# Relative-position attention with routed experts on one core: operand images in DRAM, one window transfer per quarter, and a new order of transfers

## The reference, cut to what matters

```python
attn = jnp.einsum('bhid,bhjd->bhij', q, k)
attn = attn + jnp.take_along_axis(qL, idx, axis=-1)          # idx = clip(j - i, -31, 31) + 31
attn = attn + jnp.swapaxes(jnp.take_along_axis(kL, idx, axis=-1), 2, 3)
attn = jax.nn.softmax(attn, axis=-1)
out = jnp.einsum('bhij,bhjd->bhid', attn, v)
# plus segment sums of attn by distance, times rpe_v_table; then w_proj and b_proj
```

## Time and profile before

| | us |
|---|---|
| median of 3 runs | 1705.66 (1693.27 to 1722.01) |
| the profiled execution | 1722.62 |
| its span, first to last instruction | 1720.6 |
| PE busy | 1439.5 (84%) |
| DVE busy | 1142.8 (66%) |
| ACT busy | 802.8 (47%) |
| POOL busy | 537.8 (31%) |

### The profile page before, as it was taken

The page is one execution under the profiler, slowest core; times in us unless marked ns, Lnnn a source line. Parts: engine busy times, 40 slices in busy tenths (PEclk is TensorE's granted clock), DMA queues, the critical chain, the costliest instruction groups (busy, mean ns, idle before and its releaser), DMA issues.

```text
span 1720.6 us, 69484 instructions
## 1 busy us (share of the span) xinstructions
PE 1439.5 (84%) x29626; PEld 962.7 (56%) x29626; DVE 1142.8 (66%) x2468; ACT 802.8 (47%) x1408; POOL 537.8 (31%) x557
## 2 busy tenths in 40 slices
PE   3792788888888889888898888889898888888887
PEld 1341355555555566555567555555565555555565
DVE  7782667777777677677644666665765766665672
ACT  1341245555555455444531545554554555454554
POOL 3462111222222222212333333333333433332333
PEclk9995578888998888888965988886987998888999
DMA  3553656665565555455544656665655665556552
GB/s 86 146 165 121 188 164 187 192 192 177 172 189 172 179 166 169 150 178 159 183 147 116 206 158 175 173 175 169 181 172 148 191 179 169 158 166 173 168 135 87
DMA packets 271582, 283.20 MB, mean 165 GB/s; under 512 B 55033, under 2 KB 205682, under 8 KB 271456
## 3 DMA queue, kind: packets, MB, share of 16 engines
q1 hardware_dynamic: 259984, 274.86, 52.5%
q0 software_dynamic: 11472, 6.83, 2.8%
HBM read 171.49 MB, written 112.36 MB: 165 GB/s over the span
## 4 chain that ended last, share of the span: by engine, by line
PE 50%; DMA 17%; DVE 12%; issue 9%; POOL 5%; SPq 4%; ACT 2%; DVEq 1%; another core or an unknown queue 0%; POOLq 0%; ACTq 0%
PE PS L721 43%; DMA dq_s<-dq_d 9%; DMA dq_d<-dq_e 7%; DVE tops L1505 6%; PE PS L992 5%; POOL ajp L681 3%; DVE dq_s L1546 2%; POOL ajp L679 2%; SPq L424 1%; SPq L478 1%; ACT PT L1190 1%; SPq L545 1%; PE PS L977 1%; PE PS L953 1%; ACT dq_e L1209 0%
## 5 line engine op out<-in xcount | busy, mean ns | idle before, releaser
L1505 DVE TRANSPOSE_TENSOR_REDUCE tops<-PS 128x16 f32<-128x512 f32 x1024 | 697.1, 701 | 377.2 <-PE PS L721 349.7
L1190 ACT ACTIVATE PT<-PS 128x512 f32<-128x512 f32 x1024 | 591.8, 596 | 569.2 <-PE PS L721 561.2
L721 PE MATMUL PS<-Q,K 73*32 73x512 bf16 (+28 forms) x11904 | 714.3, 348 | 140.8 <-issue 83.1
L721 PEld LDWEIGHTS PS<-Q,K 73*32 73x32 bf16 (+1 forms) x11904 | 322.1, 105 | 357.3 <-issue 171.1
L662 POOL COPY WP<-PT 128x768 f32<-128x768 f32 x128 | 105.3, 822 | 954.9 <-PE PS L721 940.8
L721 PE MATMUL PS<-PT,Vst 128*9 128x256 f32 (+7 forms) x7552 | 361.0, 308 | 2.6 <-issue 1.9
L721 PE MATMUL PS<-WT,eye 96*32 96x96 bf16 (+2 forms) x4352 | 294.8, 218 | 1.5 <-issue 1.3
L721 PEld LDWEIGHTS PS<-PT,Vst 128*9 128x9 f32 x7552 | 192.5, 98 | 84.9 <-issue 20.9
L721 PEld LDWEIGHTS PS<-WT,eye 96*32 96x32 bf16 x4352 | 185.8, 106 | 28.7 <-issue 3.2
L992 PE MATMUL PS<-ident,dq_s 127*128 127x127 f32 x512 | 108.6, 351 | 64.4 <-DMA dq_s<-dq_d 61.5
L681 POOL TENSOR_TENSOR ajp<-dq_s,ajp 128x508 bf16<-128x508 f32 x128 | 147.6, 1153 | 10.5
(11 more groups left out here) (207 smaller groups left out, 1051.8 us busy)
## 6 DMA issues: line engine op xcount, KB each, us to landing
aj_d<-ajp SPq DMA_DIRECT2D x64, 768.0 KB
WT<-aj_d SPq DMA_DIRECT2D x768, 64.0 KB, 2.0
dq_d<-dq_e SPq DMA_DIRECT2D x64, 512.0 KB
dq_s<-dq_d SPq DMA_DIRECT2D x64, 512.0 KB
TOE<-toe_d SPq DMA_DIRECT2D x33, 768.0 KB
Q<-q_stack SPq DMA_DIRECT2D x128, 96.0 KB
K<-k_stack SPq DMA_DIRECT2D x128, 96.0 KB
q_stack<-PT SPq DMA_DIRECT2D x24, 256.0 KB, 2.5
```

The costliest lines, as they stand in the source:

```text
L721: return pe.matmul(o, l, r, start=start, stop=stop, skip_group_check=True)
L1190: act.activation(PT[:, TILE + N * J + 512 * half:TILE + N * J + 512 * half + 512], PS[:, 2 + u % 2, :], ACT.Exp).then_inc(s2_read, 1)
L1505: dve.tensor_reduce(tops[:, (h + 1) % 2, s // 2, 16 * (s % 2):16 * (s % 2) + 16], PS[:, s % 2, :].rearrange("p (c i) -> p c i", i=TILE), A ...
```

## The change

1. **Row images.** `q_img` and `k_img` replace the stacks and the far tables. Each holds 60 rows per head, among them rows of ones and of products, in the order in which the operands `Q1`, `K1`, `Q2`, `K2` need them. A pass's rows are now two transfers of 60 rows, not five, and ACT issues them, at slots 1 and 7. The stores of the prologue are 16 transfers a group instead of 10. Constant rows are written once.
2. **Windows.** `aj_d` is laid out so that the three parts stand in one sheared image with a row pitch of 1056. A window quarter is one transfer of 96 rows instead of three of 32. `aj_d` is filled with zeros in the prologue. The store of `ajp` becomes three transfers, one for each part, each with the shape 4x32x1024 in DRAM.
3. **Distance products.** PE makes the product with `tabq` at slot 4 instead of 11, and the transposes of `dq_s` at slot 8 instead of 5. The transposes of `Oev` move from slot 9 to 11. `dq_d` has two buffers. `tabq` and `tabk` are loaded for every second head.
4. **SP's order** is now: TOE, quarter 2, `mparts`, the store of `dq_e`, quarter 3, `Qd`, `Ka`, quarter 0, the three stores of `ajp`, `dq_s`, quarter 1.

```diff
-        q_stack = dram("q_stack", [H * HD, COMBOS, T], BF16)
-        k_stack = dram("k_stack", [H * HD, COMBOS, T], BF16)
-        q_far = dram("q_far", [H, 6, T], BF16)
-        k_far = dram("k_far", [H, 6, T], BF16)
+        q_img = dram("q_img", [H, IMAGE, T], BF16)
+        k_img = dram("k_img", [H, IMAGE, T], BF16)
...
-        dq_d = dram("dq_d", [P, DROW])
+        dq_d = dram("dq_d", [2, P, DROW])
...
-        aj_d = dram("aj_d", [3, 3, P, N], BF16)
+        aj_d = dram("aj_d", [3, 4 * WIN * PITCH], BF16)
...
+            each = 3 * 4 * WIN * PITCH // P
+            for at in range(0, each, 2 * N):
+                n = min(2 * N, each - at)
+                sp.dma_start(rows(aj_d, at, [[each, P], [1, n]]), Z[:, :].bitcast(BF16)[:, 0:n]).then_inc(zeros_out, 16)
...
+                for img, row in ((q_img, 48), (q_img, 57), (k_img, 51), (k_img, 54)):
+                    sp.dma_start(img[:, row:row + 3, tok], ones).then_inc(ones_out, 16)
...
-                for part in range(3):
-                    sp.dma_start(WTb[TILE * part:TILE * part + TILE, t % PAIR, :, 2 * q:2 * q + 2, :].rearrange("p s j n -> p s (j n)"),
-                                 shear(t % 3, part, 2 * q, 2)).then_inc(wt_in[q], 16)
+                shear = rows(aj_d, (t % 3) * 4 * WIN * PITCH + TILE - 1 + 2 * P * q, [[PITCH - 1, WIN], [WIN * PITCH, 4], [1, 2 * P]])
+                sp.dma_start(WTb[0:WIN, t % PAIR, :, 2 * q:2 * q + 2, :].rearrange("p s j n -> p s (j n)"), shear).then_inc(wt_in[q], 16)
...
-                    sp.dma_start(aj_d[t % 3].rearrange("n p x -> p n x"), ajp[:, :, :, :].rearrange("p n j d -> p n (j d)")).then_inc(aj_out, 16)
+                    for part in range(3):
+                        sp.dma_start(rows(aj_d, (t % 3) * 4 * WIN * PITCH + part * TILE * (PITCH - 1), [[WIN * PITCH, 4], [PITCH, TILE], [1, N]]),
+                                     ajp[:, part, :, :].rearrange("p j d -> p (j d)")).then_inc(aj_out, 16)
+                if on(4) and h != hm - 1:
+                    load_distances(h + 4)
...
+            def load_rows(h, Qx, Kx, rows_in):
+                (b, hh), r = place(h), h % PAIR
+                tok = slice(b * N, b * N + N)
+                act.dma_start(Qx[ROW_S:ROWS, r, :], q_img[hh, :, tok]).then_inc(rows_in, 16)
+                act.dma_start(Kx[ROW_S:ROWS, r, :], k_img[hh, :, tok]).then_inc(rows_in, 16)
...
+                    if s == 1 and on(2):
...
+                        load_rows(h + 2, Q1, K1, rows1_in)
+                    if s == 7 and on(1):
...
+                        load_rows(h + 1, Q2, K2, rows2_in)
```

More of the change, by code:

```diff
@@ L41 @@
 DIST = 4 * TILE - 1
-ROW_M = 64
-ROW_L = 73
+ROW_M = 8
+ROW_S = 11
+ROW_L = 65
 ROW_K = 73
-ROWS = 79
-FAR = ROWS - ROW_M
+ROWS = 71
+IMAGE = ROWS - ROW_S
 LOW = DIST - 1
@@ L444, in _ @@
             sp.wait_ge(toe_out, 48)
-            sp.wait_ge(pads_set, 2)
+            sp.wait_ge(ones_out, 16 * 8)
+            sp.sem_inc(images_ready, 1)
             sp.wait_ge(psum_zeroed, 1)
[L448 to L455, removed]
             def load_dq(h):
@@ L465, in load_aj, with load_distances @@
                 tok = slice(b * N, b * N + N)
-                sp.dma_start(Ka[0:48, :], k_stack[hh * HD:hh * HD + HD, :, tok].rearrange("d n t -> (d n) t")).then_inc(ka_in, 16)
-                sp.dma_start(tabk[0:48, :], tab_stack[hh * HD:hh * HD + HD, :, 1, :].rearrange("d n p -> (d n) p")).then_inc(ka_in, 16)
+                wait(sp, aj_psum, 2 * h)
+                sp.dma_start(Ka[0:48, :], k_img[hh, 0:48, tok]).then_inc(ka_in, 16)
+                if h % 2 == 0:
+                    sp.dma_start(tabk[0:48, :], tab_stack[hh * HD:hh * HD + HD, :, 1, :].rearrange("d n p -> (d n) p")).then_inc(ka_in, 16)
+            def load_distances(h):
+                sp.wait_ge(dq_out, 16 * (h + 1))
+                wait(sp, aj_parts, 2 * h)
+                sp.dma_start(dq_s[:, :], rows(dq_d, (h % 2) * P * DROW + 1, [[DROW + 1, P], [1, N]])).then_inc(dq_in, 16)
             def load_windows(t, q):
@@ L495, in iteration @@
                                  rows(own, own.offset, [[HD, P], [1, SPAN * HD]])).then_inc(toe_in, 16)
[L496 to L502, removed]
+                if h == hm:
+                    load_distances(h + 3)
                 load_windows(h + 1, 2)
@@ L509, in iteration @@
                                      mparts[:, n, :]).then_inc(mrow_in, 16)
[L510 to L513, removed]
+                if on(4):
+                    sp.wait_ge(dq_copied, h + 5)
+                    wait(sp, aj_psum, 2 * (h + 3))
+                    sp.dma_start(dq_d[h % 2, :, 64:64 + N], dq_e[:, :]).then_inc(dq_out, 16)
                 load_windows(h + 1, 3)
-                if on(4):
-                    wait(sp, aj_psum, 2 * (h + 4))
+                if on(5):
+                    load_dq(h + 5)
+                if on(4) and h + 4 > 0:
                     load_aj(h + 4)
-                if on(1):
-                    if h >= 0:
-                        sp.wait_ge(s2_ready, SLOTS * h + 1)
-                    load_rows(h + 1, Q2, K2, rows2_in)
+                load_windows(h + 2, 0)
                 if h - hm in (3, 9, 15):
@@ L561, in iteration @@
                     load_w2(sp, 0)
-                if on(4):
-                    sp.wait_ge(dq_copied, h + 5)
-                    wait(sp, aj_psum, 2 * (h + 4))
-                    sp.dma_start(dq_d[:, 64:64 + N], dq_e[:, :]).then_inc(dq_out, 16)
                 load_windows(h + 2, 1)
+            load_dq(0)
+            load_aj(0)
             steps = iterations(sp, iteration)
```

125 lines of the change are left out of this document (73 added, 52 removed).

## The result

The changed kernel takes 2271.1 us (median of 4 runs, 2268.8 to 2281.2), the kernel before 1713.8 us beside it: a ratio of 1.337, with a 95% interval of 1.327 to 1.348. The forecast was 2025 us, with a range up to 2180. The direction and the place of the wait were right. The size was not, by 246 us.

What follows compares the result with a forecast made beforehand. PE bounded the kernel, with 61.5 us of waits for dq_s. The new circle's 12.1 + 7.2 + 8.0 = 27.3 us a head against 22.4, times 62, is 304 us, plus 15 for prologue and ramp: median 2025 us, range 1760 to 2180.

Steps and rivals of the forecast that it cites:

- Transposes no longer wait for dq_s: PE's transposes at L992, moved to slot 8: the stall for dq_s should vanish, worth at most 61.5 us.
- The store goes to four engines, and quarter 1 is late in nearly every head: Stores of ajp take 8.2 us instead of 2.0; quarter 1 is late by about 6.6 or 4 us; chance 0.82.
- The circle sets the period: In the loop: aj_parts, stores, quarter 1, slot 4, slot 8, L992, aj_parts, 27.3 us a head instead of 22.4.
- aj_parts to slot 4 (landing of quarter 1): SP's queue in each head: store 8.2, dq_s 1.4, quarter 0.5 and landing latency 2.0 us, together 12.1 us.
- slot 4 to the transposes: PE from slot 4 to slot 8: 7.2 us at half clock with the product now there, 4.9 at full clock.
- transposes to aj_parts: From L992 to SP's store of ajp: 8.0 us, or 9.4 if the half-speed stretch is not over by then.
- a period outside 24.4 to 29.2 us: Named sign on the head's period in the loop: outside these bounds the sum would be wrong in size.
- The prologue: Before the loop: zeros, ones and 15 more issues take 12 us, with 3 in the ramp 15 us (0 to 25).
- hidden beside PE's work on the group: In the prologue, the six more issues per group were taken to cost nothing, beside PE's work.
- Rows through ACT: taken as 0: Four row-load issues a head move to ACT, 1.8 us a head; hidden by its idleness, bounds 0 and 112 us.
- The blocked queue holds up more than quarter 1: Rival: ACT's row loads or mparts are held behind the stores too; 29.2 us a head, 2148 us; chance 0.12.
- Spread over 16 engines: Rival: the store of ajp stays at 2.0 us, nothing new stalls in the loop; 1676 us, not slower; chance 0.16.

Runs made afterwards that it cites:

- run 1: The changed kernel with the store of ajp as four transfers, one per block, so 32 rows are outermost in DRAM: 1935.3 us, ratio 1.137.
- run 2: The changed kernel with each of the three stores of ajp cut in two, so the outermost dimension is 2: 2751.7 us, ratio 1.616.
- run 4: The kernel before with only its store of ajp split in three, four blocks outermost: 2135.7 us, ratio 1.254.
- run 17: The changed kernel with 57 more rows of zeros, so 128 and 122 partitions are contracted: 2120.8 us.
- run 11: The kernel before with row images and ScalarE's row loads, and the lines of ones written from 128 partitions in 12 transfers: 1813.6 us, ratio 1.055.
- run 9: The kernel before with only the row images and the rows loaded through ScalarE's queue at slots 1 and 7: 1831.1 us.
- run 16: The changed kernel with 8 more rows of zeros, so 79 and 73 partitions are contracted: 2260.0 us, ratio 1.312.
- run 12: Run 11 with 8 more rows of zeros, so 79 and 73 partitions are contracted as in the kernel before: 1758.0 us, ratio 1.019.
- run 14: Run 11 with the two row loads of each pass issued by SyncE and no DMA on ScalarE's queue: 1791.7 us, ratio 1.047.
- run 3: The changed kernel with SP asking for window quarter 1 ahead of the three stores of ajp: 2189.1 us, ratio 1.285.
- run 5: The changed kernel with the old aj_d layout, one store of ajp, three transfers per window quarter and no zero fill: 1885.2 us, ratio 1.095.
- run 10: The kernel before with only the new slots, SP's new order and the second half of dq_d that they need: 1772.3 us.

## Why the prediction was right in direction and wrong in size

*Transposes no longer wait for dq_s: right.* One wait of 15.9 us in the ramp is left.

*The store goes to four engines, and quarter 1 is late in nearly every head: right.* Runs 1, 2 and 4 show it from both sides; the 0.27 share and the 96 GB/s are the ones forecast. The 60 waits of 313.6 us in all and the clock of 0.711 were among the signs named as well.

*The circle sets the period: right.* Its three terms, as means over 55 heads of the changed kernel, and over 57 of run 17. The first is counted from SP's first store of ajp to the end of PE's wait:

| term | forecast | changed kernel | run 17 |
|---|---|---|---|
| aj_parts to slot 4 (landing of quarter 1) | 12.1 | 15.3 | 15.2 |
| slot 4 to the transposes | 7.2 | 7.4 | 6.0 |
| transposes to aj_parts | 8.0 | 8.1 | 7.1 |
| sum (of the unrounded) | 27.3 | 30.8 | 28.4 |

Run 17 tests the circle by itself. The clock shortens only the two terms in which PE works, by 2.4 us, and 62 x 2.4 = 149 us is about what it gained (150 by the medians, 141 by the profiled executions). The landing did not move.

*The step that failed is the first term of the sum, "from aj_parts to the landing of quarter 1: 12.1 us".* It was 15.3, and 3.2 x 62 = 198 us, most of the 246. By the prediction's own sign, a period outside 24.4 to 29.2 us, the sum was wrong in size. I had taken 24.1 GB/s per engine from the first moment, and nothing else on the four engines. The trace shows a slow start instead:

```profile
624.00:626.00 2.00, 2.00 (x45) 1.52 (x35) 1.56 (x6) 1.19 (x2) 0.00 (x0) 0.50 0.11 12
```

The first packet of 2048 bytes starts 1.2 us after the issue, which belongs to the latency of 2.0 us. Then 16 packets take 1.6 us (mean over the heads), where at 97 GB/s they would take 0.3; that is 1.3 of the 3.2 us. The row loads of ScalarE, 246 KB in each of these intervals, stand on the same four engines too; if a quarter of their bytes does, that is an estimated 0.6 us. TOE is hardly a cause: with it the term is 15.4 us (30 heads), without it 15.1 (27). Over 1 us is left open, and none of these parts was tried by a run.

*The rest of the 246 us.* The span grew by 546 us and not by 319, which is 227 too much: 192 in the loop's period (30.4 instead of 27.3), 25 in the prologue, and 13 in the head with the experts (107.0 us instead of 94.3), which was not in the sum, less 2 at the end. The other 19 are in the level: the forecast took 17 us off to come from the profiled execution to the median, and for the changed kernel the median lies 2 us above it.

*The prologue was the second: 39.8 us instead of 15.* The timeline of SP shows where:

```profile
55.99 4.22 SPq L436 DMA_DIRECT2D aj_d<-PT  x5
60.32 2.10 SPq L443 DMA_DIRECT2D q_img<-Q  x2
62.46 3.28 SPq L443 DMA_DIRECT2D k_img<-Q  x2
65.78 3.81 SPq L443 DMA_DIRECT2D q_img<-Q  x2
69.63 3.80 SPq L443 DMA_DIRECT2D k_img<-Q  x2
73.48 6.74 SPq L398 DMA_DIRECT2D q_img<-PT  x6
```

The zeros ran at the 386 GB/s that I took and a little more. The ones read 16 partitions of Q2 and ran at about 100, so SP stood 13.0 us in four rows; 1.6 MB at the 386 GB/s of the sum are 4.1:

```profile
66.00:70.00 4.00, 0.00 (x0) 0.00 (x0) 0.00 (x0) 0.00 (x0) 0.00 (x0) 0.50 0.96 102
```

The stores of the images thus begin 19.0 us later than those of the stacks did (73.48 against 54.49). They end 27.8 us later, 8.8 more, with six issues of 0.6 us where three were. I had those "hidden beside PE's work on the group". The other 12.0 us are in the ramp, where PE waits 16.2 us for windows instead of 4.9; I had 3. What SP's delay costs PE is one wait:

```profile
PE PS L728 <- ACT TOE L1160: 28.6, 1, 28.6
```

How the prologue divides is read from the trace. Of runs, only run 11 bears on it: it mends the ones alone, and its first head begins 6.4 us earlier than in run 9.

*What was not in the sum at all:* the contraction. The dropped rows of zeros are in the constants of the diff, and the earlier trace rows have the 73. I had costed them at nothing without saying so. In this sum it did little harm (11 us by the medians, run 16), since the circle hid it. With the circle gone it is some 56 us (run 12) of the 161 that stay.

*"Rows through ACT: taken as 0", bound 112.* Run 14 puts it at 22 us, not clear of the noise, in a kernel without the circle. "PE has time to wait" was right for the changed kernel as far as the missing waits for PT show.

*The rivals.* "The blocked queue holds up more than quarter 1" (2148) was nearest in time, but not in mechanism: the waits for the maxima appear only when quarter 1 is moved up (run 3). "Spread over 16 engines" was given 1676; run 5, in which the store is, takes 1885. Of these 209 us the slots have 55 and the row images 114 (runs 10 and 9). So the forecast for that case was wrong in direction as well: it said "not slower", and run 5 is 9.5% slower.

## What to carry to other kernels

Read the outermost dimension of both sides of every transfer, and the number of partitions it reads, before its bytes; then ask what else passes over the engines that it lands on, because a circle through such a store can cost more than is won elsewhere (422 us for the store alone, run 4, against 61.5 us of waits that the change could win). Where a profile shows the same busy time for PE with fewer matmuls done, look at the granted clock before looking for a wait, and try rows of zeros in the contraction: 32 of them, at no cost in instructions or transfers, made this kernel 3.6% faster. Take a change apart from the side of the kernel before as well: here the parts about added up (114 and 55 for 161), while mending the changed kernel piece by piece gave ever smaller returns.

## What the runs showed of the hardware that I had not expected

- TensorE's granted clock, at nearly equal busy time (430 to 439 of the 500 us from 1000 to 1500), rose with the number of contracted partitions: 0.79 with 71, 0.86 with 79, 0.92 with 111 (in the kernel before), 0.95 with 128. The added rows held zeros in K. Which property of the matmul counts (rows, weights, toggling, place in the array) was not tried.
- The rate of a store rose with the number of partitions that it read on the chip: 102 GB/s with 16 (the ones), 200 to 225 with 32 (run 1), 386 with 128. In each case the DMA share was 0.96 or more, so the engines were taken all the same. The three stores differ in shape too, and no run changed the partitions alone.
- Four engines at work alone kept the rate of 24 GB/s each that sixteen have (0.27 and 96 GB/s), but only after a slow start: 16 packets in the first 1.6 us. The one store of 128 rows before shows none (382 GB/s from 1 us after its issue at 438.28).
